# Weights loaded in groups as they are needed, and the ternary weights made between the first products

## What is computed

```python
x = x + attention0(ln(x))    # 16 heads of 16, scores scaled by 1/4; a maximum for each of two key blocks of 256, and no rescaling between them
x = x + ffn0(ln(x))          # ternary layer below, hidden width 1024
x = x + attention1(ln(x))    # q, k, v with biases, ordinary softmax
x = x + trees(ln(x))         # 8 trees of 255 nodes: silu of the nodes on the chosen path, times W_out

def bitlinear(x, w):
    scale = clip(mean(abs(w), axis=1), 1e-5)
    tern = clip(round(w / scale), -1, 1)
    return x @ ((w + (tern - w)) * scale).T
h = bitlinear(x, w_fc) + gate * (x @ v.T @ fast_b.T @ u.T)
ffn0 = bitlinear(relu(h) ** 2, w_proj)
```

## Time and profile before

| | us |
|---|---|
| median of 3 runs | 3346.56 (3345.4 to 3348.39) |
| profiled execution, its own time | 3350.38 |
| its span in the profile | 3348.3 |
| busy: TensorE, VectorE, ScalarE, GpSimd | 3053.1, 2225.5, 1915.2, 911.7 |
| first instruction that computes on loaded data | 75.37 |
| first exponential (L524) | 175.25 |

### The profile page before, as it was taken

How to read it: one execution, slowest core, us unless ns; L and a number is a source line. 1 busy time by engine, 2 the same in 40 slices (tenths; PEclk the granted TensorE clock), 3 DMA queues, 4 the chain that set the end, 5 groups by cost and what they waited for, 6 DMA issues and landing times.

```text
span 3348.3 us, 51469 instructions
## 1 busy us (share of the span) xinstructions
PE 3053.1 (91%) x20499; PEld 1392.4 (42%) x20499; DVE 2225.5 (66%) x4099; ACT 1915.2 (57%) x2559; POOL 911.7 (27%) x1206
## 2 busy tenths in 40 slices
PE   0489999999999999999999999999999999999999
PEld 0124355242543436333363434524254343633336
DVE  0785866758566675767667586675856667576764
ACT  0265664747557474565746566474754748456574
POOL 0012323141331414214141232314233141421413
PEclk9689999999999999999999999999999999999999
DMA  3000000000010001000010000100001000100000
GB/s 119 21 22 20 22 27 33 22 20 22 31 38 12 23 19 50 28 2 30 24 39 28 18 24 21 39 22 20 22 29 39 12 22 19 47 28 6 30 18 20
DMA packets 92703, 91.08 MB, mean 27 GB/s; under 512 B 15757, under 2 KB 89877, under 8 KB 92453
## 3 DMA queue, kind: packets, MB, share of 16 engines
q1 hardware_dynamic: 92465, 87.79, 7.7%
HBM read 17.48 MB, written 8.39 MB: 8 GB/s over the span
## 4 chain that ended last, share of the span: by engine, by line
PE 63%; DVE 25%; ACT 5%; SPq 3%; issue 2%; POOL 1%; DMA 1%; DVEq 0%
PE ps L995 13%; PE ps L1040 11%; PE ps L1065 11%; PE ps L1271 8%; DVE nmax L756 8%; DVE nmax L753 8%; PE ps L1001 5%; PE ps L1020 4%; PE ps L1242 3%; PE ps L1051 3%; ACT probs L524 3%; SPq L263 2%; DVE h L734 1%; DVE hT L739 1%; PE ps L1008 1%
## 5 line engine op out<-in xcount | busy, mean ns | idle before, releaser
L524 ACT ACTIVATE probs<-ps 128x1024 f32<-128x1024 f32 x1024 | 1042.8, 1025 | 376.1 <-PE ps L1051 371.9
L1040 PE MATMUL ps<-kst,qst 48*128 48x512 f16 x2048 | 719.1, 394 | 114.0 <-DVE nmax L753 50.5
L753 DVE TENSOR_REDUCE nmax<-ps 128x2 f32<-128x512 f32 x1024 | 651.0, 685 | 196.3 <-PE ps L1040 190.8
L756 DVE TENSOR_REDUCE nmax<-ps 128x1 f32<-128x512 f32 x1024 | 651.2, 685 | 175.7 <-PE ps L1040 172.2
L1051 PE MATMUL ps<-qst,kst 54*128 54x512 f16 x2048 | 697.3, 391 | 5.0 <-ACT probs L524 5.0
L1065 PE MATMUL ps<-probs,vn 128*32 128x512 f32 (+1 forms) x5184 | 577.6, 519 | 6.6 <-ACT oT L512 6.6
L1040 PEld LDWEIGHTS ps<-kst,qst 48*128 48x128 f16 x2048 | 164.4, 93 | 734.1 <-DVE nmax L753 308.0
L420 POOL TENSOR_TENSOR probs<-probs 127x512 f16<-127x512 f32 (+1 forms) x256 | 292.4, 1164 | 519.5 <-ACT probs L655 519.5
L655 ACT ACTIVATE probs<-probs 127x512 f16<-127x512 f32 (+1 forms) x256 | 161.7, 632 | 350.2 <-DVE probs L949 346.8
L1271 PE MATMUL ps<-wout,probs 127*128 127x256 f16 (+1 forms) x3072 | 357.2, 273 | 0.0
L995 PE MATMUL ps<-hT,win 128*127 128x512 f16 (+1 forms) x1536 | 354.3, 380 | 2.7 <-ACT probs L631 2.7
(11 more groups left out here) (117 smaller groups left out, 3282.0 us busy)
## 6 DMA issues: line engine op xcount, KB each, us to landing
qst<-parts SPq DMA_DIRECT2D x384, 64.0 KB, 2.6
kst<-parts SPq DMA_DIRECT2D x384, 64.0 KB, 2.6
x<-in_x SPq DMA_DIRECT2D x16, 512.0 KB, 3.9
probs<-x SPq DMA_DIRECT2D x16, 512.0 KB, 3.0
out<-probs SPq DMA_DIRECT2D x16, 512.0 KB, 3.0
qst<-nrow SPq DMA_DIRECT2D x256, 12.0 KB
qst<-in_winT SPq DMA_DIRECT2D x1, 2040.0 KB
oT<-in_wfcT SPq DMA_DIRECT2D x1, 1024.0 KB
```

Of the source, the lines that this page charges most:

```text
L524: nc.scalar.activation(probs[:, g % 2, 2 * hf:2 * hf + 2, s % G, :], ps[:, 2 + 2 * hf:4 + 2 * hf, :], ACT.Exp).then_inc(exp_rd, 1)
L753: nc.vector.tensor_reduce(nmax[:, u, 2 * tt + half, :, slot], bank[tt % 2].rearrange("p (a s) -> p a s", s=BLK), AX.X, ALU.max, negate=Tru ...
L756: nc.vector.tensor_reduce(nmax[:, u, 2 * tt + half, 0, slot:slot + 1], bank[tt % 2], AX.X, ALU.max, negate=True).then_inc(max_rd, 1)
L1040: mm(bank[tt % 2], qst[lo:hi, ai % 2, e // 2, tt * P:(tt + 1) * P], kst[lo:hi, ai % 2, e // 2, :], start=True, stop=True).then_inc(max_ps, 1)
```

## The change

The loads are grouped by when they are needed, each group on a semaphore of its own: first the input x of sequence 0 with the two identity matrices and q, k, v of layer 0 (`first_loads`); then `wfc`; then x of sequence 1; then the rest of the first feed-forward (`ffn_loads`) and the constant rows; and, after the stacking DMAs of the first sequence, the remaining attention weights and biases, `win`, and the tree output weights. The 127 rows of the last are loaded as 112 and 15. The raw weights now lie in `probs` (32 slots), scratch of the ternary work in `wout`, `wfc`, `oT`, `hT[1]`, `qst`.

The first sequence is normalised before anything of the ternary weights, and so is the second. The means over `wfc` come between query/key unit 1 and value unit 0, those over `wproj` and the low-rank products after query/key unit 3. VectorE does the ternary work for `wfc`, 16 of the 28 lead maxima, the ternary work for `wproj`, the low part of `wfc`, and then the other 12.

Of the twelve low parts VectorE keeps q, k, v of layer 0 and `wfc`. The other eight go to GpSimd, as a subtraction of two tensors in SBUF; since that instruction has no scale, ScalarE writes the raw weight times 64 in place as well (`w_scaled`), eight instructions more. GpSimd also fills `vn`. ScalarE makes both halves of `wout` after the first `row_read` and before its first exponential. Its first write to the slots that hold `win` and `wout` raw waits for `w_lo_pool` 8.

```diff
-        raw_out = kst[:].rearrange("p q a s -> p (q a s)").bitcast(F32).rearrange("p (a l e) -> p a l e", a=PAR, l=2)
+        raw_out = flat(24, 32).rearrange("p (a l e) -> p a l e", a=PAR, l=2)
...
-        loads = [
-            (raw_fc, t["wfcT"].rearrange("(k p) n -> p k n", p=P)),
-            (raw_pr, t["wprT"].rearrange("(k p) n -> p k n", p=P)),
...
-            (raw_in, t["winT"].rearrange("(k p) n -> p k n", p=P)),
-            (raw_out[0:INNER, :, 0, :], t["woutT"].rearrange("(a n) e -> n a e", n=NODES)[0:INNER]),
-            (raw_out[0:LEAVES, :, 1, :], t["woutT"].rearrange("(a n) e -> n a e", n=NODES)[INNER:NODES]),
-            (bqk[:], t["bqk"]), (bv[:], t["bv"]),
-            (bin_[:], t["bin"].rearrange("p (a n) -> p a n", n=2)),
-            (anc[:], t["anc"].bitcast(F16)), (bo[:], t["bo"]), (thr[:], t["thr"]),
-        ]
-        ALL_IN = 16 * (len(loads) - PAIR)
...
+        attn_loads = [(raw_attn[:, i], w.rearrange(by_k, p=P)) for i, w in enumerate(names)]
+        first_loads = [(idf[:], t["idf"]), *attn_loads[0:3], (idb[:], t["idb"].bitcast(F16))]
+        fc_load = (raw_fc, t["wfcT"].rearrange(by_k, p=P))
+        ffn_loads = [(fbs, t["fast_b"]), (uTs, t["uT"]), (vs, t["v"]), (gate[:], t["gate"]),
+                     (raw_pr, t["wprT"].rearrange(by_k, p=P))]
+        other_loads = [*attn_loads[3:], (bqk[:], t["bqk"]), (bv[:], t["bv"]), (bin_[:], t["bin"].rearrange("p (a n) -> p a n", n=2)),
+                       (anc[:], t["anc"].bitcast(F16)), (bo[:], t["bo"]), (thr[:], t["thr"])]
+        out_rows = t["woutT"].rearrange("(a n) e -> n a e", n=NODES)
+        winT_load = (raw_in, t["winT"].rearrange(by_k, p=P))
+
+        even = INNER // 16 * 16
+        tree_loads = [(raw_out[0:even, :, 0, :], out_rows[0:even]), (raw_out[0:LEAVES, :, 1, :], out_rows[INNER:NODES]),
+                      (raw_out[even:INNER, :, 0, :], out_rows[even:INNER])]
+
...
+        attn_parts = [(raw_attn[:, 4 * l + i], w[l][:, HI], w[l][:, LO]) for l in range(2) for i, w in enumerate((wq, wk, wv, wo))]
+        w_parts = attn_parts + [
             (raw_in, *(win[:, p].rearrange("p k a n -> p k (a n)") for p in (HI, LO))),
+            (raw_fc, wfc[:, HI], wfc[:, LO]),
             (raw_out[0:INNER, :, 0, :], wout[0:INNER, HI, :, 0, :], wout[0:INNER, LO, :, 0, :]),
             (raw_out[0:LEAVES, :, 1, :], wout[0:LEAVES, HI, :, 1, :], wout[0:LEAVES, LO, :, 1, :]),
-            (raw_fc, wfc[:, HI], wfc[:, LO]),
         ]
+        OWN, IN, FC = 3, 8, 9
+        POOLED = len(w_parts) - OWN - 1
         TERN = 18
...
-            for dst, src in loads[:-PAIR]:
-                sp.dma_start(dst, src).then_inc(w_in, 16)
-            for q in range(PAIR):
-                sp.dma_start(*loads[len(loads) - PAIR + q]).then_inc(y_out[q], 16)
-
             def load(q, wrap):
                 sp.dma_start(x[q][:], t["x"][bass.ds(wrap * PAIR + q, 1)].rearrange("o (t p) d -> p (o t) d", p=P)).then_inc(x_in[q], 16)
 
             load(0, 0)
+            for dst, src in first_loads:
+                sp.dma_start(dst, src).then_inc(first_in, 16)
+            sp.dma_start(*fc_load).then_inc(fc_in, 16)
             load(1, 0)
-            sp.wait_ge(w_lo, len(w_parts))
+            for dst, src in ffn_loads:
+                sp.dma_start(dst, src).then_inc(ffn_in, 16)
...
+            for dst, src in other_loads:
+                sp.dma_start(dst, src).then_inc(attn_in, 16)
+            sp.dma_start(*winT_load).then_inc(winT_in, 16)
+            for dst, src in tree_loads:
+                sp.dma_start(dst, src).then_inc(tree_in, 16)
             rows_up(0, 0, 0)
...
         def _(pool):
             nc.gpsimd.memset(mhalf[:], -0.5).then_inc(pool_set, 1)
             nc.gpsimd.memset(zero[:], 0.0).then_inc(pool_set, 1)
+            nc.gpsimd.memset(vn[:], 1.0).then_inc(vn_set, 1)
             pool.wait_ge(pool_set, 2)
-            pool.wait_ge(w_in, ALL_IN)
+
+            def weights_low(i):
+                raw, hi, lo = w_parts[i]
+                pool.wait_ge(w_hi, i + 1)
+                pool.wait_ge(w_scaled, i - OWN + (i < FC))
+                nc.gpsimd.tensor_tensor(lo, raw, hi, ALU.subtract).then_inc(w_lo_pool, 1)
 
             def rstd_of(b, ph):
                 pool.wait_ge(ln_mv, (b * PHASES + NORM[ph]) * 7 + 7)
                                             mhi[0:rows, a % 2, leaf, :], ALU.subtract).then_inc(mlo_sb, 1)
 
             rstd_of(0, 0)
-            for c in range(4):
-                qk_low(0, c)
+            qk_low(0, 0)
+            qk_low(0, 1)
+            rstd_of(0, 1)
+            qk_low(0, 2)
+            qk_low(0, 3)
+            for i in range(OWN, IN):
+                weights_low(i)
             split_maxima(0, 0, 0)
-            rstd_of(0, 1)
+            for i in (IN, *range(FC + 1, len(w_parts))):
+                weights_low(i)
             for b in range(PAIRS):
                 more = b + 1 < PAIRS
...
-            act.wait_ge(w_in, ALL_IN)
-            nc.scalar.activation(wabs, raw_fc.rearrange("p k n -> p (k n)"), ACT.Abs).then_inc(abs_done, 1)
-            act.wait_ge(mean_ps, 2)
-            nc.scalar.activation(wabs, raw_pr.rearrange("p k n -> p (k n)"), ACT.Abs).then_inc(abs_done, 1)
-            act.wait_ge(g1_ps, 2)
...
-            for i, (raw, hi, lo) in enumerate(w_parts):
-                if i == len(w_parts) - 1:
-                    act.wait_ge(tern, TERN)
-                nc.scalar.activation(hi, raw, ACT.Copy, scale=WS).then_inc(w_hi, 1)
+            def weights_high(i):
+                nc.scalar.activation(w_parts[i][1], w_parts[i][0], ACT.Copy, scale=WS).then_inc(w_hi, 1)
+                if i >= OWN and i != FC:
+                    nc.scalar.activation(w_parts[i][0], w_parts[i][0], ACT.Copy, scale=WS).then_inc(w_scaled, 1)
 
...
-                if ph == 0 and s == 4 and hf == 1:
+                if b == 0 and ph == 0 and s == 4 and hf == 0:
+                    act.wait_ge(w_lo_pool, POOLED)
+                if b and ph == 0 and s == 4 and hf == 1:
                     for q in range(PAIR):
-                        act.wait_ge(y_out[q], b * 16 + 16)
+                        act.wait_ge(y_out[q], b * 16)
...
+            act.wait_ge(first_in, 16 * len(first_loads))
+            for i in range(OWN):
+                weights_high(i)
             hT_high(0, 0, 0)
             hT_high(0, 0, 1)
+            act.wait_ge(fc_in, 16)
+            nc.scalar.activation(wabs, raw_fc.rearrange("p k n -> p (k n)"), ACT.Abs).then_inc(abs_done, 1)
             qk_read(0, 0, 0)
             qk_read(0, 0, 1)
+            act.wait_ge(vn_set, 1)
             values(0, 0, 0)
             values(0, 0, 1)
             qk_read(0, 0, 2)
             qk_read(0, 0, 3)
+            act.wait_ge(ffn_in, 16 * len(ffn_loads))
+            act.wait_ge(mean_ps, 2)
+            nc.scalar.activation(wabs, raw_pr.rearrange("p k n -> p (k n)"), ACT.Abs).then_inc(abs_done, 1)
+            act.wait_ge(g1_ps, 2)
+            nc.scalar.activation(g1, ps[0:RANK, 0:2, :].rearrange("p a s -> p (a s)"), ACT.Copy).then_inc(g1_sb, 1)
+            act.wait_ge(attn_in, 16 * len(other_loads))
+            for i in range(OWN, IN):
+                weights_high(i)
+            act.wait_ge(winT_in, 16)
+            weights_high(IN)
+            act.wait_ge(tern, TERN)
+            weights_high(FC)
             row_read(0, 0)
+            act.wait_ge(tree_in, 16 * len(tree_loads))
+            for i in range(FC + 1, len(w_parts)):
+                weights_high(i)
+            act.wait_ge(w_lo_pool, IN - OWN)
...
-            dve.wait_ge(w_in, ALL_IN)
...
-            nc.vector.memset(vn[:], 1.0).then_inc(vn_set, 1)
...
-            dve.wait_ge(tern, TERN)
-            for i, (raw, hi, lo) in enumerate(w_parts):
-                dve.wait_ge(w_hi, i + 1)
-                nc.vector.scalar_tensor_tensor(lo, raw, WS, hi, ALU.mult, ALU.subtract).then_inc(w_lo, 1)
...
+            def tern_fc():
+                dve.wait_ge(mean_ps, 2)
+                nc.vector.tensor_scalar_max(scl, ps[:, 2:4, :].rearrange("p a s -> p (a s)"), 1e-5).then_inc(tern, 1)
...
+                dve.wait_ge(tern, 8)
+                nc.vector.tensor_tensor(raw_fc, raw_fc, bc(scl, KD, F0), ALU.mult).then_inc(tern, 1)
...
+            def tern_pr():
+                dve.wait_ge(mean_ps, 3)
...
+                nc.vector.tensor_tensor(wpt[:], v3(tgt, M0, D), v3(tlt, M0, D), ALU.subtract).then_inc(tern, 1)
...
+                dve.wait_ge(tern, TERN)
+
+            def weights_low(i):
+                raw, hi, lo = w_parts[i]
+                dve.wait_ge(w_hi, i + 1)
+                nc.vector.scalar_tensor_tensor(lo, raw, WS, hi, ALU.mult, ALU.subtract).then_inc(w_lo, 1)
+
+            nc.vector.memset(onesf, 1.0 / D).then_inc(ones_set, 1)
+            nc.vector.memset(onesp, 1.0 / F0).then_inc(ones_set, 1)
             arrived(0, 0)
             moments(0, 0)
             normalise(0, 0)
+            for i in range(OWN):
+                weights_low(i)
```

(95 more changed lines are left out.)

85 lines of the change are left out of this document (35 added, 50 removed).

## The result

The changed kernel takes 3254.1 us, median of 4 runs (3248.7 to 3259.9), against 3347.5 before (4 runs). The ratio is 0.971, with a 95% interval of 0.9695 to 0.9726: 93.4 us less. The forecast was 3251. The profiled execution took 3248.72 us and is the fastest of the four; against the 3350.38 of before it is 101.7 us shorter, and the sum had said 95.3. One execution of the kernel before, run beside the first three experiments, took 6394 us and is left out of all medians and ratios here.

What follows compares the result with a forecast made beforehand. The start was taken as a serial chain of loads, VectorE work and one head start of maxima; -91.3 us to the first exponential and -4.0 behind it gave 3255.1 us profiled, median 3251, range 3240 to 3268.

Steps and rivals of the forecast that it cites:

- the sum: Whole kernel: 91.3 us from an earlier first exponential plus 4.0 behind it, 95.3 us off the profiled 3350.38.
- The load over one engine: Start, tree weights: a load of 127 rows goes over one DMA engine, at 0.07 of the DMA share and 25 GB/s.
- Rival 3: Tree loads: the 112 rows do not spread, 896 KB at 22 GB/s take 40.7 us; kernel 3273 us; chance 0.07.
- T: Start of the first query/key unit, at 139.74 us before; forecast at 14.0 us.
- Stacking and loads: SyncE's queue in the start: free at 34.8 us, eleven loads in 10.9, the last landed at 49.6.
- The shared path: VectorE's two-SBUF-input subtractions and GpSimd exclude each other: wfc's low half waits for win's until 71.0, costing 6.2 us.
- Rival 1: No exclusion worth its name: wfc's low half runs at 64.8, first exponential at 77.7, kernel 3245 us; chance 0.20.
- Rival 2: GpSimd's win subtraction gets in before wproj's last two-input subtraction; wfc's low half ends 79.9, not 73.3; 3258 us; chance 0.13.
- From there to E: From the end of wfc's low half at 73.3 us, through maxima, row tile and four ScalarE wout copies, to 83.9.
- E: Start of the first exponential, at 175.25 us before; forecast at 83.9 us, 91.3 us earlier.
- Behind E: Second exponential, 5.9 us after the first before: 4.0 us saved (2.7 to 4.5); later pairs unchanged.
- Rival 4: TensorE's clock stays at its lower level after a gappier start, making the kernel slower, e.g. about 3370 us; chance 0.02.

Runs made afterwards that it cites:

- the first three experiments: Before kernel with the 127-row load cut in two, 3305.8 us; that plus two load semaphores, 3289.7; changed kernel with 127 rows in one piece, 3281.2.
- win_late: Changed kernel, with GpSimd starting the low half of win only after VectorE's low half of wfc; 3256.0 us in one run.
- bias_early: Changed kernel, with VectorE's two bias products ahead of the ternary work on wproj; 3260.1 us in one run.
- rows_127: Changed kernel, with the inner tree rows loaded as 127 in one piece again; 3281.2 us, median of 4 runs.
- after_third: The changed kernel again, unaltered, run beside a later reordered kernel on the same chip; 3253.6 us, median of 5 runs.

## Why the prediction was right, point by point

- **The load over one engine**: right, and larger than anything else. Taking it away alone gave 43.9 us; putting it back in the changed kernel cost 26 us. Rival 3 did not occur: 112 rows do spread. (Its 896 KB at 22 GB/s are 41.7 us and not 40.7; nothing hangs on it.)
- **T** came at 13.4, forecast 14.0. The term not shown by any row, GpSimd's fill of the value tile, took 3.51 us, the lower of the two bounds, and delayed nothing.
- **Stacking and loads**: SyncE was free at 34.4 (34.8), but the issue behind the 127-row table held it for 2.47 us, not 4.9, the ten others took 0.29 to 0.59 each, so the last weight was usable at 45.65 instead of 49.6. This term was mis-sized most, by 4 us, and with it win's copies ended at 58.0 (62.9).
- **GpSimd's win subtraction**: 9.48 us against 8.1, since it began 1.7 us before VectorE's subtraction was done. Alone it takes 7.91 (win_late), near the slope of the earlier trace rows. It ended at 67.6, forecast 71.0.
- **The shared path**, the term that decided: right in its mechanism, but half as large as forecast. The low half of `wfc` stands with 5.35 us, and with 2.29 when GpSimd is idle: 3.1 us of waiting where the sum had 6.2. It was wanted at 64.4, as forecast (64.8), and waited less because the win subtraction ended 3.4 earlier. In wfc's ternary work, too, a comparison and a subtraction of two SBUF tensors took 3.25 and 3.13 instead of 2.29, beside two low splits of GpSimd that took 5.17 together; 1.8 us where 0 to 2.3 were allowed. Rival 1 fell. The Trainium skill (SBUF — State Buffer, "Who interferes with whom") has the rule; these rows agree with it, both ways round.
- **Rival 2**, priced at 6.6 us with 5.9 of cover, had 0.58 of cover in truth: win's copies ended 4.9 earlier (54.41 + 3.59) and VectorE was 0.6 later. bias_early took it away with 1.2 us of other work. The cover was the weak number of the prediction, not the mechanism.
- **From there to E**: 12.2 us (69.77 to 81.94), forecast 10.6. The forecast laid the end on ScalarE's copies. They end at 80.0; what came last was a bias product of two elements that took 2.50 us beside GpSimd, and 0.16 with GpSimd idle (rows_127). The prediction had not placed the two bias products at all: here a small product from SBUF to SBUF waits too, where I had charged only instructions with two SBUF inputs. It is a hand-over that the prediction had not seen, smaller than the 5 to 20 us that it set aside for one.
- **How near the numbers are** is in part luck. The low half of `wfc` ended 3.5 us before its forecast and the stretch behind it was 1.6 longer, which leaves E at 81.94 against 83.9. The median is 3 us over the forecast of 3251, the profiled execution 6.4 under its 3255.1: the four executions range from 3248.7 to 3259.9.
- **Behind E**: the second exponential came 2.75 us after the first, instead of 5.93, 3.2 saved of 4.0 forecast. The 13th came 21.9 after E instead of 28.2, so 6.3 were saved there in this execution, and 3.6 in after_third; the forecast did not have the rest.
- **The steady part** was taken as unchanged. It is: 3037.8 to 3040.0 us in three profiles of the changed kernel, 3039.5 before.
- **Rival 4** did not occur: the granted clock is 0.50 over the window from 37.5 to 85.0 us and back at 1.00 over that from 110 to 260.

## What to carry to other kernels

Look first at the row count of a load that is slow: 127 rows ran at 22 GB/s for over 40 us, and cut in 112 and 15 they vanished. When work goes to GpSimd, price it by which VectorE instructions stand beside it: between two subtractions in SBUF the later one waits until the other is done, so a long GpSimd instruction belongs beside reductions from PSUM, and an instruction of two elements can cost as much as a large one. And a gap of half a microsecond in such a race is no cover; an edit of 1.2 us ahead of it made the next large step 5.7 us later.
